# Two graph layers on one core: the second norm's output goes from the vector engine through SBUF and the DMA transpose, the second attention runs two graphs behind

## The chip, the cores and the metric

The kernel runs on one core of a Trainium2 chip, in one launch. The time is device time in microseconds (us), the median of several runs. The engines of the core work in parallel, each on its own queue in program order: TensorE (PE; its weight loads are listed as PEld), VectorE (DVE), ScalarE (ACT), GpSimd (POOL) and SyncE (SP), whose queue only issues DMAs here. They wait for each other on semaphores alone; nothing else orders them.

## What is computed

There are 32 graphs of 256 nodes with 512 features, float32. Each goes through a multi-head attention layer with an adjacency mask and then through a second, single-head graph attention, both behind a layer norm with relu and both added to their input:

```python
h = jnp.maximum(_layernorm(x), 0.0)
# L0: 16 heads of 32
q, k, v = heads(h @ Wq + bq), heads(h @ Wk + bk), heads(h @ Wv + bv)
scores = jnp.einsum('bhqd,bhkd->bhqk', q, k) * scale
scores = jnp.where(adj[:, None] == 0, -jnp.inf, scores)
x = x + (softmax(scores) @ v) @ Wo + bo
h = jnp.maximum(_layernorm(x), 0.0)
# L1: alpha from feature @ wq and feature @ wk
alpha = jnp.maximum((h @ wq) @ (h @ wk).T, 0.0) * (adj != 0)
x = x + softmax(alpha, axis=1) @ (h @ weight)
```

## The kernel before

**Tiles.** A graph is two row tiles of 128 nodes by 512. Every float32 factor is split into a high and a low float16 part, and a product is made of three matmuls (high by high, high by low, low by high). ACT writes the high part, DVE the low part (input minus high); for the attention weights POOL writes the low part (line 1115). `wm` is the product of the two second-layer attention matrices, made once at the start, so alpha is h2 wm h2^T: `g0`, `g1` make wm^T h2^T, `al` makes alpha, `hw0`, `hw1` make h2 times the weight, `av0`, `av1` the weighted sum.

**Stages.** The loop body (one for each graph t, all engines) has 16 steps, one for each head u. `weigh(u)` (PE lines 483 and 485, eight pairs of short products) stands at the start of step u+1; behind it a step holds the dense tiles that the table `DENSE` gives it, about as much PE work in each. `ROLE` says for which graph a tile is made in body t (0: t, 1: t+1, -1: t-1). `BANK` gives each tile one of three PSUM banks (`ring`); PE waits until DVE has finished the tile that had the bank before. `scores` of four heads stand at the ends of steps 11, 15, 3, 7. The first two bodies (t = -1 and 0) and the last ones are written out; 2 to 29 are a hardware loop. In body 0 the tiles of graph -1 are missing, and their places are used to make `wm` and the merged bias (`merge`, `merged_low`).

**A head.** DVE masks the scores (line 864, `mask`, four or five steps ahead), ACT takes the exponential (625) and the high part (638), POOL the low part (1115), and SP issues a DMA transpose of both parts (355, `turned`) at step u-1 of its own queue. PE's `weigh(u)` waits for its landing. DVE then sums high and low parts (877 and 879, `sum_parts`) for each pair of heads; `weigh` of the next even head waits for that, because it reuses the bank.

**The second norm.** In steps 2 and 3 DVE adds the products `wo0`, `wo1` to `x1` (963) and takes their statistics (883). In step 4 it makes mean and deviation (889, 907 to 911) and the normalised rows `work` (916, two passes). In step 5 PE turns them with eight float32 transposes through the identity (518, tiles `h2_0`, `h2_1`) between the halves of `v1`; ACT (649) and DVE (921) make relu's high and low part of them out of PSUM. `g0` follows in step 6.

**The first norm** goes another way: POOL normalises (1137), ACT and DVE split in SBUF (694, 921 `half`), and SP turns both parts with two DMA transposes (367, `transpose_h1`) in step 6, behind the `turned` of head 7. ACT issues the load of the next input `xa` (766) in step 5.

**The second softmax.** `al` ends in step 11. DVE masks alpha (981), takes the maximum (996), ACT the exponential (707), DVE the reciprocal (1004, 1007), ACT and DVE the parts `e` (718, 1012) in step 12; `av0`, `av1` stand in steps 14 and 15 of the same body, and DVE adds `x1` to them into `xo` (990), which SP stores in step 1 of the next body.

## Time and profile before

| what | value |
|---|---|
| median of 3 runs | 1568.2 us (1566.75 to 1570.06) |
| the profiled execution, as timed | 1570.8 us |
| its span in the profile | 1569.0 us |
| PE busy | 1504.6 us (96%) |
| DVE, ACT, POOL busy | 1247.9, 1128.3, 1064.8 us |
| DMA transposes | 512 of `turned`, 64 of `h`, all from SP |
| PE's granted clock, mean | 0.992 |

The rows further down are of four kinds. The page has one line for each engine with its busy time, share and number of instructions. A timeline row is: start in us, length in us, engine, line and operation, names written and read, shape, number of instructions merged, and in brackets the idle time of the engine before it and what ended it. A row of the windows view has a stretch, its length, each engine's busy time and number of instructions, the granted PE clock (1.00 is 2.4 GHz, 0.50 is 1.2 GHz), the busy share of the DMA engines and GB/s. A DMA issue row has what is moved, the issuing queue, the number, and the median us from issue to landing.

### The profile page before, as it was taken

The numbers are of one execution on the slowest core, as the hardware profiler recorded it, in microseconds if no ns is written. First come the engines' busy times: TensorE is split into PE (matmuls) and PEld (weight loads), VectorE is DVE, ScalarE is ACT, GpSimd is POOL, SyncE is SP. The second block draws the span as 40 slices with busy tenths as digits, with TensorE's granted clock in tenths as the row PEclk, the third lists the DMA queues.
The fourth block names the chain that finished last, engine by engine and source line by source line (L and its number), as shares of the span: only waits on it lengthen the run. The fifth ranks groups of instructions, "written<-read, shape, count | busy, mean of one in ns | idle before, by whom it ended". The sixth has DMA issues, their size and how long they took to land.

```text
span 1569.0 us, 50846 instructions
## 1 busy us (share of the span) xinstructions
PE 1504.6 (96%) x16561; PEld 1106.7 (71%) x16561; DVE 1247.9 (80%) x4042; ACT 1128.3 (72%) x2477; POOL 1064.8 (68%) x1478
## 2 busy tenths in 40 slices
PE   2889999999999999999999999999999999999996
PEld 1557777777777777777777777777777777777753
DVE  6778888887887878788888878888887888888763
ACT  2567777777777777777777777777777777777761
POOL 2466767777677777767677776777776777777650
PEclk9999999999999999999999999999999999999998
DMA  7647777667667766666776766777676677767760
GB/s 241 135 95 132 133 163 160 152 136 152 138 138 166 160 144 143 144 136 148 166 157 141 152 140 134 154 160 159 135 158 136 133 161 160 153 135 159 125 119 16
DMA packets 656198, 226.28 MB, mean 144 GB/s; under 512 B 611488, under 2 KB 627872, under 8 KB 656160
## 3 DMA queue, kind: packets, MB, share of 16 engines
q1 hardware_dynamic: 636848, 188.57, 59.1%
q10 hardware_dynamic: 19312, 37.23, 8.5%
q8 instruction: 21, 0.34, 0.1%
q14 instruction: 17, 0.14, 0.0%
HBM read 57.94 MB, written 16.78 MB: 48 GB/s over the span
## 4 chain that ended last, share of the span: by engine, by line
POOL 35%; issue 34%; PE 22%; DVE 4%; ACT 2%; DMA 1%; POOLq 1%; SPq 0%; ACTq 0%; DVEq 0%
PE ring L408 18%; POOL wv_raw L1115 16%; POOL heads_out L1149 6%; POOL x L1172 4%; POOL keep L1181 3%; POOL far L1190 3%; POOL xa L1137 1%; PE score L464 1%; PE pv L483 1%; DMA turned<-wv_raw 1%; POOL newton L1133 1%; PE ring L518 1%; PE pv L485 0%; DVE wk_raw L864 0%; DVE tops L785 0%
## 5 line engine op out<-in xcount | busy, mean ns | idle before, releaser
L1115 POOL TENSOR_TENSOR wv_raw<-wk_raw,wv_raw 128x512 f16<-128x512 f32 x512 | 608.0, 1190 | 362.8 <-ACT wv_raw L638 358.5
L625 ACT ACTIVATE wk_raw<-wk_raw,least 128x256 f32<-128x256 f32 x1024 | 459.0, 497 | 6.8 <-DVE least L864 6.8
L864 DVE CUSTOM_DVE_ANT_0 wk_raw<-score,far,undo_score 128x256 f32<-128x256 f32 x1024 | 444.0, 478 | 7.1 <-issue 5.1
L638 ACT ACTIVATE wv_raw<-wk_raw 128x512 f16<-128x512 f32 x512 | 320.5, 626 | 8.6 <-issue 4.5
L483 PEld LDWEIGHTS pv<-val,turned 128*128 128x128 f16 x2048 | 149.7, 97 | 67.4 <-issue 43.9
L483 PE MATMUL pv<-val,turned 128*128 128x65 f16 x2048 | 185.9, 192 | 10.8 <-DMA turned<-wv_raw 7.0
L408 PE MATMUL ring<-wv_hi,h 128*128 128x256 f16 x1024 | 189.3, 273 | 0.0
L408 PE MATMUL ring<-h,wq_hi 128*128 128x256 f16 x1024 | 176.3, 274 | 7.6 <-DVE wk_lo L827 7.6
L1149 POOL TENSOR_TENSOR heads_out<-o_sum,o_rcp 128x64 f32<-128x64 f32 x512 | 153.0, 320 | 42.6 <-DVE o_sum L879 42.6
L485 PE MATMUL pv<-val,turned 128*128 128x33 f16 x2048 | 178.1, 179 | 0.0
L408 PE MATMUL ring<-h,wk_hi 128*128 128x256 f16 x1024 | 176.6, 274 | 0.0
L485 PEld LDWEIGHTS pv<-val,turned 128*128 128x128 f16 x2048 | 136.1, 96 | 15.3 <-issue 1.3
L408 PE MATMUL ring<-h_hi,wm_hi 128*128 128x256 f16 x512 | 140.4, 274 | 2.0 <-DVE h_lo L921 1.6
L408 PE MATMUL ring<-h_hi,wm_lo 128*128 128x256 f16 x512 | 140.6, 275 | 0.0
L408 PE MATMUL ring<-h,wq_lo 128*128 128x256 f16 x512 | 140.5, 274 | 0.0
L408 PE MATMUL ring<-h_lo,wm_hi 128*128 128x256 f16 x512 | 140.5, 274 | 0.0
L408 PE MATMUL ring<-h,wk_lo 128*128 128x256 f16 x512 | 140.4, 274 | 0.0
L408 PE MATMUL ring<-wv_lo,h 128*128 128x256 f16 x512 | 140.0, 273 | 0.0
L408 PEld LDWEIGHTS ring<-h,wq_hi 128*128 128x128 f16 x1024 | 93.4, 98 | 24.5 <-DVE wk_lo L827 7.7
L408 PEld LDWEIGHTS ring<-wv_hi,h 128*128 128x128 f16 x1024 | 100.2, 98 | 14.2
L464 PE MATMUL score<-stage 32*128 32x256 f16 x3072 | 107.4, 270 | 1.7 <-DVE stage L942 1.2
L939 DVE SCALAR_TENSOR_TENSOR stage<-ring,bias_q,stage 128x256 f16<-128x256 f32 x128 | 61.6, 481 | 58.5 <-ACT stage L660 54.8
(151 smaller groups left out, 3570.6 us busy)
## 6 DMA issues: line engine op xcount, KB each, us to landing
xin<-x_dram ACTq DMA_DIRECT2D x32, 512.0 KB, 3.8
out_dram<-xo SPq DMA_DIRECT2D x32, 512.0 KB, 3.7
xa<-x_dram ACTq DMA_DIRECT2D x31, 512.0 KB, 4.2
adj_in<-adj_dram SPq DMA_DIRECT2D x32, 256.0 KB, 2.9
turned<-wv_raw SPq DMA_TRANSPOSE x512, 3.2
adjt_in<-adj_t_dram SPq DMA_DIRECT2D x32, 256.0 KB, 3.1
wq_raw<-wq_dram SPq DMA_DIRECT2D x2, 512.0 KB, 7.0
wk_raw<-wk_dram SPq DMA_DIRECT2D x2, 512.0 KB, 8.6
```

The costliest lines, as they stand in the source:

```text
L408: last = nc.tensor.matmul(dst, a, b, start=(k == 0 and s == 0), stop=(k == tiles - 1 and s == 2))
L464: last = nc.tensor.matmul(score[i][:, q * NODES:(q + 1) * NODES], stage[rows, g % 2, of_q, q * P:(q + 1) * P], stage[rows, g % 2, of_k, :] ...
L483: nc.tensor.matmul(pv4[:, slot, 0:VCOLS], turned[:, u % DEEP, q, 0, k, :], val[:, k, u, 0:VCOLS], start=(k == 0), stop=False)
L485: last = nc.tensor.matmul(pv4[:, slot, HEAD:VCOLS], turned[:, u % DEEP, q, 1, k, :], val[:, k, u, HEAD:VCOLS], start=False, stop=(k == QT ...
L625: last = nc.scalar.activation(probs[:, at, q, :], probs[:, at, q, :], ACT.Exp, bias=least[:, at, q:q + 1], scale=-1.0)
L638: nc.scalar.activation(halves[:, at, :, 0, :], probs[:, at, :, :], ACT.Copy).then_inc(hi["p"], 1)
L864: last = nc.vector.tensor_tensor_reduce(out=probs[:, at, q, :], in0=score[u % GROUP][:, q * NODES:(q + 1) * NODES], in1=far[:, q, :], scal ...
L939: nc.vector.scalar_tensor_tensor(out=stage[:, k % 2, 1, :], in0=src[:, 0:NODES], scalar=bias_q[:, k:k + 1], in1=stage[:, k % 2, 0, :], op0 ...
L1115: nc.gpsimd.tensor_tensor(halves[:, at, :, 1, :], probs[:, at, :, :], halves[:, at, :, 0, :], ALU.subtract).then_inc(lo["p"], 1)
L1149: last = nc.gpsimd.tensor_tensor(dst, o_sum[:, pair % 2, q:q + 3:2, :], o_rcp[:, pair % 2, q:q + 3:2].unsqueeze(2).broadcast_to([P, 2, HEAD]),
L1172: last = nc.gpsimd.tensor_tensor(x1[:, q, :], xin[:, q, :], out_bias[:], ALU.add)
L1181: last = nc.gpsimd.tensor_scalar(keep[:, q, :], adjt_in[:, q, :], 0, 0, ALU.is_equal, ALU.is_equal)
```

## The change

- **Second norm.** `work` is no longer turned by PE. ACT writes relu's high part of it (two instructions, step 4) and DVE its low part (two instructions, step 5) into `half2` in SBUF, and SP turns them with two DMA transposes (`transpose_h2`, step 5, between `turned` of head 6 and of head 7). `g` and `hw` wait for the landing of both (`h2_in`).
- **Table.** `v1` is whole in step 5; `av0`, `av1` stand in step 6 and belong to graph t-2; `g0` starts in step 7 as `g0a`; `g0b`, `g1a` in 8, `g1b`, `qk0a` in 9, `qk0b`, `hw0a` in 10, `hw0b`, `ot0` in 11, `al` whole in 12, `qk1` in 13, `v0a`, `hw1a` in 14, `hw1b`, `v0b` in 15. The softmax of alpha stands in step 13.
- **Residual.** SP copies `x1` to `xo` by DMA in step 12; DVE adds the attention's product to `xo` in place. The store moves from step 1 to step 8.
- **Buffers.** `g` and `hw` live in the space of the raw `wk1_t`.
- **Entry and end.** SP loads `wq` and `wv`, ACT loads `wk`; the first norm of graph 0 is made on DVE instead of POOL; eight small matmuls stand before the first product; the first product waits for the split of `wq` alone; the merges and scale searches of body 0 and the weight splits are dealt to other steps; the last two bodies have tables of their own (`DENSE_LAST`, `DENSE_END`).

```diff
-    ["v1a", "h2_0", "h2_1", "v1b"],
-    ["g0"],
-    ["g1a"],
-    ["g1b", "hw0a"],
-    ["hw0b", "qk0a"],
-    ["qk0b", "ala"],
-    ["alb", "ot0"],
-    ["hw1"],
+    ["v1"],
+    ["av0", "av1"],
+    ["g0a"],
+    ["g0b", "g1a"],
+    ["g1b", "qk0a"],
+    ["qk0b", "hw0a"],
+    ["hw0b", "ot0"],
+    ["al"],
     ["qk1"],
-    ["v0a", "av0"],
-    ["av1", "v0b"],
+    ["v0a", "hw1a"],
+    ["hw1b", "v0b"],
 ]
...
 AL_STEP = step_of("al")
+SOFTMAX_STEP = AL_STEP + 1
...
-VAR2 = 4
+VAR2, TURN2_STEP = 4, 5
...
-ADJ_STEP, STORE_STEP = 0, 1
+ADJ_STEP, STORE_STEP, KEEP_X_STEP = 0, 8, 12
...
             sp.dma_start(xa[:], x_v[0, :, :, :]).then_inc(xa_in, 16)
+            for half in range(2):
+                load_raw(sp, "wq", half)
...
+            def transpose_h2(b):
+                if started(b - 1):
+                    sp.wait_ge(mm["hw"], count(b - 1, 2, 1))
+                    sp.wait_ge(mm["al"], count(b - 1, 1, 0))
+                for q in range(QT):
+                    sp.wait_ge(lo["h2"], count(b, QT, q))
+                    settle(sp, sp_settled)
+                    sp.dma_start_transpose(
+                        h2[:, :, :, q * P:(q + 1) * P].rearrange("p h d n -> p (h d) n"),
+                        half2[:, q, :, :].rearrange("p h d -> p (h d)")).then_inc(h2_in, 16)
+
+            def keep_residual(b):
+                sp.wait_ge(added, count(b, 2, 1))
+                if started(b - 1):
+                    sp.wait_ge(stored, count(b - 1, 16, 15))
+                sp.dma_start(xo[:], x1[:]).then_inc(kept, 16)
...
                         transpose_probs(*head)
                     if s == TURN1_STEP and nxt:
                         transpose_h1(n)
+                    if s == TURN2_STEP and prev:
+                        transpose_h2(p)
+                    if s == KEEP_X_STEP and prev:
+                        keep_residual(p)
...
-                    pe.wait_ge(lo["h2"], count(b, 2, k))
+                    pe.wait_ge(h2_in, count(b, QT, QT - 1) * 16)
...
-                    for d in range(KT):
-                        last = nc.tensor.transpose(dst[:, d * P:(d + 1) * P],
-                                                   work[:, k, d * P:(d + 1) * P], ident[:])
-                    last.then_inc(mm["h2"], 1)
...
+            def second_half(q, b):
+                act.wait_ge(normed[1], count(b, QT, q))
+                if started(b - 1):
+                    act.wait_ge(h2_in, count(b - 1, QT, QT - 1) * 16)
+                nc.scalar.activation(half2[:, q, 0, :], work[:, q, :], ACT.Relu
+                                     ).then_inc(hi["h2"], 1)
...
+            def second_half(q, b):
+                dve.wait_ge(hi["h2"], count(b, QT, q))
+                relu_low(half2[:, q, 1, :], work[:, q, :], half2[:, q, 0, :], lo["h2"])
...
-                    if k == 0 and started(b - 1):
-                        dve.wait_ge(stored, count(b - 1, 16, 15))
+                    if k == 0:
+                        dve.wait_ge(kept, count(b, 16, 15))
                     nc.vector.scalar_tensor_tensor(out=xo[:, k, :], in0=src[:],
-                                                   scalar=undo_final[:, 0:1], in1=x1[:, k, :],
+                                                   scalar=undo_final[:, 0:1], in1=xo[:, k, :],
...
+                    if s == VAR2 + 1 and prev:
+                        for q in range(QT):
+                            second_half(q, p)
```

How the queues stand after it, at two places of the loop body. The first is SP's queue in steps 5 to 7; `turned` is a head's transpose, `h1` and `h2` the two norms'. The other instructions of the queue are the issuing engine's own waits and registers. Before, from head 7 on:

```order
L355 DMA_TRANSPOSE turned<-wv_raw 128x8x128 [waits lo_p,mm_pv]
L362 ISA
L363 ISA [waits mm_qk]
L365 ISA [waits mm_v]
L367 DMA_TRANSPOSE h1<-half1 128x8x128 [waits lo_h1]
L365 REGISTER_ALU
L367 DMA_TRANSPOSE h1<-half1 128x8x128 [waits lo_h1]
L348 REGISTER_ALU
L355 DMA_TRANSPOSE turned<-wv_raw 128x8x128 [waits lo_p,mm_pv]
```

The same place now:

```order
L412 ISA [waits mm_al,mm_hw]
L414 DMA_TRANSPOSE h2<-half2 128x8x128 [waits lo_h2]
L412 REGISTER_ALU
L414 DMA_TRANSPOSE h2<-half2 128x8x128 [waits lo_h2]
L384 REGISTER_ALU
L391 DMA_TRANSPOSE turned<-wv_raw 128x8x128 [waits lo_p,mm_pv]
L398 ISA
L399 ISA [waits mm_qk]
L401 ISA [waits mm_v]
L403 DMA_TRANSPOSE h1<-half1 128x8x128 [waits lo_h1]
L401 REGISTER_ALU
L403 DMA_TRANSPOSE h1<-half1 128x8x128 [waits lo_h1]
```

The two turns of `h2` stand ahead of head 7's, so four turns of norms instead of two lie between the low part of head 7 and the turn of head 8.

The second place is DVE's queue around the second softmax. `wk_raw,least<-score` is half a head's mask, `work<-ring,keep` the mask of alpha, `o_sum` a pair's sum. Before:

```order
L981 SCALAR_TENSOR_TENSOR work<-ring0,keep 128x512
L996 TENSOR_REDUCE l1_max<-work 128x2
L999 TENSOR_SCALAR l1_max<-l1_max,undo 128x2
L954 REGISTER_ALU
L955 TENSOR_TENSOR heads_t_lo<-ring1,heads_t_hi 128x512
L874 REGISTER_ALU
L877 RECIPROCAL o_rcp<-pv 128x4
L879 TENSOR_REDUCE o_sum<-pv 128x128
L1004 TENSOR_SCALAR l1_sum<-l1_sum 128x2
L1007 RECIPROCAL l1_rcp<-l1_sum 128x2
```

Now:

```order
L954 RECIPROCAL o_rcp<-pv 128x4
L956 TENSOR_REDUCE o_sum<-pv 128x128
L933 ISA
L937 REGISTER_ALU
L941 ISA wk_raw,least<-score0,far,undo_score 128x256
L941 ISA least 128x1
L941 ISA wk_raw,least<-score0,far,undo_score 128x256
L941 ISA least 128x1
L1058 SCALAR_TENSOR_TENSOR work<-ring2,keep 128x512
L1073 TENSOR_REDUCE l1_max<-work 128x2
L1076 TENSOR_SCALAR l1_max<-l1_max,undo 128x2
L1081 TENSOR_SCALAR l1_sum<-l1_sum 128x2
```

The pair's sum and head 0's mask now stand ahead of alpha's mask, and nothing stands between the maximum and the sum that waits for the exponential. Behind it come the masks of heads 1 and 2, `e_lo`, `qk1`'s low parts and the sum of the pair of heads 12 and 13.

## Rows read from the trace of the kernel before

**Rows 1.** The page: span, and PE with busy time, share and instructions.

```profile
span 1569.0 us, 50846 instructions
PE 1504.6 (96%) x16561; PEld 1106.7 (71%) x16561; DVE 1247.9 (80%) x4042; ACT 1128.3 (72%) x2477; POOL 1064.8 (68%) x1478
```

**Rows 2.** Windows view of one graph's period, and all transposes of line 518.

```profile
1131.86:1177.85 45.99, 45.97 (x519) 34.17 (x518) 37.70 (x125) 34.77 (x79) 33.28 (x47) 1.00 0.69 148
...
L518 PE MATMUL ring<-ident,work x256: 272/273/331, 117.8 to 1539.6; 128*128 128x128 f32 x128
```

**Rows 3.** PE's timeline: transposes, `v1b`, then the starts of steps 6, 9, 10.

```profile
1131.86 1.28 PE L518 MATMUL ring<-ident,work 128*128 128x128 f32 x8
...
1132.98 0.27 PE L408 MATMUL ring<-wv_hi,h 128*128 128x256 f16 x1
...
1134.29 0.19 PE L483 MATMUL pv<-val,turned 128*128 128x65 f16 x1
...
1142.62 0.20 PE L483 MATMUL pv<-val,turned 128*128 128x65 f16 x1
...
1145.46 0.19 PE L483 MATMUL pv<-val,turned 128*128 128x65 f16 x1
```

**Rows 4.** DVE's timeline, steps 1 to 5 of the same body.

```profile
1123.20 0.48 DVE L939 SCALAR_TENSOR_TENSOR stage<-ring,bias_q,stage 128x256 f16<-128x256 f32 x1 [0.77 <-ACT stage L660]
...
1133.22 1.29 DVE L921 SCALAR_TENSOR_TENSOR h_lo<-ring,h_hi 128x512 f16<-128x512 f32 x2
```

**Rows 5.** Timelines of SP and ACT, DMA issues with us to landing, h's minimum/median/maximum.

```profile
1134.95 1.23 SPq L367 DMA_TRANSPOSE h<-half  x1
...
1136.37 2.60 SPq L367 DMA_TRANSPOSE h<-half  x1
...
1139.22 5.93 SPq L355 DMA_TRANSPOSE turned<-wv_raw  x4
...
1134.81 0.39 ACTq L766 DMA_DIRECT2D xa<-x_dram  x1
...
h<-half SPq DMA_TRANSPOSE x1, 4.7
...
turned<-wv_raw SPq DMA_TRANSPOSE x4, 3.3
...
DMA to landing us min/median/max: 3.3/4.8/8.1
```

**Rows 6.** Timelines of PE and DVE, from alpha's end to step 15.

```profile
1149.83 0.27 PE L544 MATMUL ring<-ident,heads_out 128*128 128x128 f32 x1
...
1159.62 0.19 PE L483 MATMUL pv<-val,turned 128*128 128x65 f16 x1
...
1150.03 0.69 DVE L981 SCALAR_TENSOR_TENSOR work<-ring,keep 128x512 f32<-128x512 f32 x1 [1.01 <-PE ring L408]
...
1153.60 0.48 DVE L864 CUSTOM_DVE_ANT_0 wk_raw<-score,far,undo_score 128x256 f32<-128x256 f32 x1 [0.18 <-issue]
...
1154.65 0.88 DVE L1012 SCALAR_TENSOR_TENSOR e_lo<-work,l_rcp,e_hi 128x256 f16<-128x256 f32 x2 [0.15 <-ACT e_hi L718]
...
1156.05 0.47 DVE L864 CUSTOM_DVE_ANT_0 wk_raw<-score,far,undo_score 128x256 f32<-128x256 f32 x1
...
1158.66 0.17 DVE L877 RECIPROCAL o_rcp<-pv 128x4 f32<-128x4 f32 x1
...
1158.75 0.39 DVE L879 TENSOR_REDUCE o_sum<-pv 128x128 f32<-128x256 f32 x1
```

**Rows 7.** PE's timeline behind a wait near the end, and the windows view there.

```profile
1522.31 0.38 PE L408 MATMUL ring<-hw_hi,e_hi 128*128 128x512 f16 x1 [2.10 <-DVE hw_lo L970]
...
1522.91:1526.32 3.41, 3.41 (x17) 1.41 (x16) 0.75 (x1) 0.00 (x0) 0.47 (x2) 0.50 0.70 66
```

**Rows 8.** Timelines of ACT, DVE and PE at the entry.

```profile
10.57 1.06 ACT L694 ACTIVATE half<-xa 128x1024 f16<-128x1024 f32 x1 [3.95 <-POOL xa L1137]
...
24.50 2.48 DVE L827 SCALAR_TENSOR_TENSOR wq_lo<-wq_raw,scale,wq_hi 128x1024 f16<-128x1024 f32 x2 [1.12 <-ACT wq_hi L618]
...
29.43 0.61 PE L408 MATMUL ring<-h,wq_hi 128*128 128x256 f16 x2 [7.61 <-DVE wk_lo L827]
```

More of the change, by code:

```diff
@@ L84 @@
 HIGH1_STEP, LOW1_STEPS, TURN1_STEP = 14, (0, 2), 6
-VAR2 = 4
+VAR2, TURN2_STEP = 4, 5
 X1_STEP, XIN_STEP, KEEP_STEP, FAR_STEP = 1, 4, 4, 11
-ADJ_STEP, STORE_STEP = 0, 1
-SPARE = [tile(name) for name in ORDER if tile(name) in ("hw0", "hw1", "g0", "g1", "al", "av0")]
+ADJ_STEP, STORE_STEP, KEEP_X_STEP = 0, 8, 12
+JOBS = {"ot1": "bias", "wo1": 0, "av0": "turn", "av1": 1, "g0": "spread", "g1": 2, "hw0": 3,
+        "al": "turn", "hw1": "spread"}
+BATCH_OF = {"av0": 2, "g0": 2, "al": 3, "hw1": 3}
+SPARE = [tile(name) for name in ORDER if tile(name) in JOBS]
+MERGES = ["bias", 0, 1, 2, 3]
+WARM = 8
 LOADS = ("wq", "wk", "wv", "wk1_t", "wq1_t", "wo", "w1")
@@ L113, in started, with deal, bank_of, order @@
     return not (isinstance(graph, int) and graph < 0)
+def deal(t):
+    if isinstance(t, int) and t >= BATCH - 1:
+        return DENSE_LAST if t == BATCH - 1 else DENSE_END
+    return DENSE
+def bank_of(name, b):
+    if isinstance(b, int) and b == BATCH - 1 and ROLE[name] == -1:
+        return BANK_END[name]
+    return BANK[name]
 def bank_before(name, t):
-    at, shift = ORDER.index(name), 0
+    def order(body):
+        return [other for step in deal(body) for other in step if not other.endswith("b")]
+    body, at = t, order(t).index(name)
     while True:
@@ L121, in bank_before @@
         if at < 0:
-            at, shift = at + len(ORDER), shift - 1
-        other = ORDER[at]
-        if BANK[tile(other)] != BANK[tile(name)]:
+            body -= 1
+            at = len(order(body)) - 1
+        other = order(body)[at]
+        graph = body + ROLE[other]
+        if bank_of(tile(other), graph) != bank_of(tile(name), t + ROLE[name]):
             continue
-        graph = t + shift + ROLE[other]
-        if t + shift == 0 and tile(other) in SPARE:
+        if body == 0 and tile(other) in SPARE:
             return other, -1 - t
-        if t + shift < -1:
+        if body < -1:
             return None, 0
@@ L444, in merge @@
                                                 stop=(k == KT - 1))
-                else:
-                    for half in range(2):
-                        wait_raw(pe, "wo", half)
-                    for k in range(KT):
-                        last = nc.tensor.matmul(dst[:], bv_wide[:, k, :], raw["wo"][:, k, :],
-                                                start=(k == 0), stop=(k == KT - 1))
                 last.then_inc(merged, 1)
@@ L606, in body @@
                             scores(g, t)
+                    if nxt and not cur and s == SCORE_STEPS[0]:
+                        spread_scale(1, 1, pv)
             for name in ORDER:
-                assert len({bank_before(name, t) for t in range(2, BATCH - 2)}) == 1
+                assert len({bank_before(name, t) for t in range(2, BATCH - 1)}) == 1
             sweep(pe, body)
@@ L766, in body @@
                         act.dma_start(xa[:], x_v[n + 1, :, :, :]).then_inc(xa_in, 16)
+            for half in range(2):
+                load_raw(act, "wk", half)
             act.wait_ge(const_ok, 2)
@@ L1049, in body @@
                         first_low(1, n)
+                    if soften and not cur:
+                        second_low(p)
                     if s == LATE_MASK and cur:
```

233 lines of the change are left out of this document (134 added, 99 removed).

## The prediction

> **What bounds the kernel now.** The page comes first: PE is busy for 1504.6 of 1569.0 us, the next engine is at 80% [rows 1]. The windows view of one graph's period says how hard that bound is: in 45.99 us PE is busy for 45.97, at the full clock, while DVE has 37.70, ACT 34.77 and POOL 33.28 us of work [rows 2]. So a period is the sum of PE's issue times, and work taken off PE shortens it as long as nobody makes PE wait. The timelines say how close the others are behind. Head 8's turn is issued at 1139.22 and lands 3.3 us later, at 1142.5 [rows 5]; the products that wait for it start at 1142.62 [rows 3]. The sum of heads 12 and 13 ends at 1159.1 and PE wants it at 1159.62 [rows 6]. Both have slack of 0.1 and 0.5 us, so the order of the small queues matters as much as PE's work.
>
> **1. The eight transposes go.** They start at 1131.86, and `v1b` behind them at 1132.98 [rows 3]: 1.12 us of PE for each graph, 32 times (256 instructions, rows 2), 36 us in all if nothing else moves. ACT's and DVE's two instructions each stay about as long (DVE's two took 1.29 us out of PSUM [rows 4]) and stay at the same place of DVE's queue (ACT's come a step earlier). The rest of the dense work is only dealt anew.
>
> **2. A wait ahead of `g0a`.** When are the parts of h2 ready? DVE's last wait before them is in step 1, for `qk2` (1123.20); from there to the two passes at 1133.22 it works without a gap [rows 4]. The change alters nothing in between, and mask 9 still stands ahead, so the low parts end at about 1133.9 and 1134.5 as before. The first turn is issued at 1133.9. What two such turns take is seen at h1: the second is issued 1.42 us after the first, itself occupies the queue for 2.60 us and lands 4.7 us later [rows 5]. There ACT's 512 KB load of `xa` was issued at 1134.81, 0.14 us ahead of the first [rows 5]; in the new order it comes behind `v1`, which now ends 1.1 us earlier, and so falls on the first h2 turn again. Landing: 1133.9 + 1.4 + 4.7 = 1140.0; with the least that any turn of h took, 3.3 us, 1138.6 [rows 5]. PE gets there as follows: step 6 begins at 1134.29 - 1.12 = 1133.17; `av0`, `av1` fill a step (2.84 us, from 1142.62 to 1145.46 [rows 3]), and head 6's short products take some 0.25 us: 1136.3. So PE stands still for 2.3 to 3.7 us in every graph, more than the 1.12 us that it saved. Behind `g0a` come 5.2 us of work until head 8's products (1142.62 - 1.12 - 1136.3).
>
> **3. The turns of heads 7 and 8.** In SP's queue the two h2 turns stand ahead of head 7's, which was ready earlier, and h1's two stand behind that. Issue times: h2 at 1133.9 and 1135.3, head 7 at 1135.3 + 2.85 = 1138.2 (the step from 1136.37 to 1139.22 [rows 5]), then h1, h1 and head 8 at about 1.5 us each (four in 5.93 [rows 5]): 1142.7, landing at 1146.0. PE could be there at 1140.0 + 5.2 = 1145.2, so the turn decides: step 9 starts at 1146.0 instead of 1142.62, 3.4 us later, the saving included. Without the collision with `xa` all of it comes some 1.4 us earlier, 2.0 us later than before. The store that now stands behind head 8's turn can hold up head 9's by a few tenths more (512 KB, as long as xa's effect at most): upper end 4.1. I take 3.4, the collision being the row that is nearest.
>
> **4. A wait in step 15.** Before, `al` ended at 1149.83 and head 14's products stood at 1159.62 [rows 6], 9.8 us later. Now `al` ends with step 12, and head 14 stands two steps behind: 2 x 2.84 = 5.7 us. DVE's chain between them, counted from the end of `al`: alpha's mask starts 0.2 behind it (1150.03) and the first head mask 3.6 behind that (1153.60), since DVE waits for ACT's exponential meanwhile; then the masks of heads 1 and 2 and `qk1`'s parts, which took from 1156.05 to 1158.66, 2.6 with 0.2 of waiting in it; `e_lo`, 0.8; the pair's sum, 0.5 [rows 6]. That is 0.2 + 3.6 + 2.4 + 0.8 + 0.5 = 7.5 us against 5.7. The head mask and `hw_lo` that stood in the old chain are gone from it, and still it is too long. PE waits 1.8 us; with ACT a little quicker or slower 1.4 to 2.0; I take 1.7. DVE's idle time before it, while `al` was running, can't be used, since its queue is in order.
>
> **5. The moved residual, the store, the buffers.** `xo` needs the copy at step 6 of the next body, ten steps after its issue; two turns of heads behind it may be late by about a microsecond each, under step 15's wait. DVE's additions keep their length. I cost this at nothing; if that cover is gone, it is up to 0.7 us a graph.
>
> **6. Entry and end.** The first product started at 29.43, behind the low parts of `wk` [rows 8]. It now needs those of `wq` alone, one group of 2.48 us less, and the first norm no longer waits 3.95 us for POOL [rows 8] but for about 1.9 us of DVE (three small and two long instructions): together 4.5 us. Body 0's merges lie better spread, 1.5. At the end the first attention product fills gaps and `hw0`, `hw1` stand under the softmax, but the turn by DMA stands in the open: -2, give or take 3. Together -8, from -14 to -2.
>
> **7. The sum.** Steps 2 to 4 apply to bodies 1 to 30 or so, taken as 30: 30 x (3.4 + 1.7) = 153. Span 1569.0 + 153 - 8 = 1714. The profiled execution was timed 1.8 above its span and 2.6 above the median, so the median should be 0.8 below: 1713 us.
>
> **A rule that speaks against the change.** Rows 3 show eight transposes by PE in 1.12 us, rows 5 two DMA turns of as much data in 6.1 us from the first issue (1.4 and 4.7). The Trainium skill, page "VectorE: DVE Perf Modes", section "Rules for kernel authors", says to turn a 128x128 tile on TensorE if the target may be PSUM, and by the DMA crossbar otherwise. By that rule the change would lose wherever the landing isn't covered; the trace agrees on the order of the two.
>
> **The rivals.**
> - **The turns are covered and PE's saving stays** (faster). For it: `av0`, `av1` and head 6 stand between, 3.1 us. It decides at `g0a`: the second turn would have to land by 1136.3, and step 9 gains only while head 8's turn is there before 1142.6. For that DVE's passes would have to come over 2.3 us earlier, and SP's four extra microseconds of queue vanish. Against it: rows 4 and 5 throughout. Time: 1569.0 - 36 - 8 - 0.8 = 1524.
> - **Only the norm's wait is there**, step 15's isn't, because some link of DVE's chain overlaps that I counted one behind the other: 30 x 3.4 - 8: 1662; without the collision too (2.0), 1620.
> - **The clock falls in each graph.** Behind an idle time of 2.10 us PE ran 3.41 us at 0.50, that is 1.2 instead of 2.4 GHz [rows 7]; an idle time of 3.7 us in each graph would cost up to 1.7 us more each. Part of it hides under head 8's turn (0.8 us of room). With 1.7 in full and the upper ends of steps 3 and 4 (4.1 and 2.0): 30 x 7.8 - 8: 1794; more likely 30 x 6: 1740. The Trainium skill, page "TensorE: Matmul & The Clock Gate", Part 1, says that PE's clock is let through at half rate when PE has been idle and in full once it is busy; by that rule this rival holds in most graphs, and rows 7 agree for one place.
> - **The change doesn't do what it says**: not likely; the order of the queues shows the transposes gone and the DMAs there.
>
> **How the numbers follow.** Both waits, with or without some clock loss, 1680 to 1775: 0.65. Only the first wait, 1620 to 1680: 0.15. Above 1775: 0.08. Between 1570 and 1620 (both much smaller than reckoned): 0.03. Covered turns, about 1524: 0.08. No change: 0.01. The range leaves out the top and everything under 1620: 1620 to 1775. A measurement can tell about 0.2%, 3 us, from no change. Faster 0.08, same 0.01, slower 0.91.
>
> **What would show it.** Right: PE idle of 2.3 to 3.7 us ahead of `g0a`, released by the DMA of h2; head 8's products released by their turn; PE idle of about 1.7 us ahead of head 14's products, released by `o_sum`; a period near 51 us; PE's clock mean under 0.99. Wrong: a period of 45 us with PE busy throughout would mean that the low parts of h2 come earlier in DVE's queue than I think, or that the turns land faster; a period of 49 that only the first wait is real.

## The result, and the profile after

| what | before | after |
|---|---|---|
| median | 1567.5 us (1563.8 to 1570.1) | 1758.0 us (1756.8 to 1759.9) |
| span of the profiled execution | 1569.0 us | 1755.9 us |
| mean period of the loop, from weigh(0) to weigh(0) | 45.98 us | 52.07 us |
| PE's granted clock, mean | 0.992 | 0.957 |

The changed kernel takes 1.121 times as long (95% interval 1.119 to 1.123). The period was read over 29 graphs from the starts of `weigh(0)` in PE's timeline.

The page of after, its line on the engines, answers [rows 1]. PE has 237 instructions fewer, and yet it is busy for longer, since part of the time its clock is halved:

```profile
span 1755.9 us, 50712 instructions
PE 1529.4 (87%) x16324; PEld 1101.4 (63%) x16324; DVE 1272.8 (72%) x4054; ACT 1130.5 (64%) x2477; POOL 1066.7 (61%) x1470
```

PE's waits of after (engine and line, releaser: us in total, times, longest). The first row holds two waits of each graph, the second one:

```profile
PE pv L543 <- DVE o_sum L956: 91.9, 63, 4.9
PE ring L465 <- DMA h<-half: 79.8, 32, 7.2
```

The windows view of one period, against [rows 2]: 46.62 of 51.77 us are busy, where before it was 45.97 of 45.99.

```profile
1092.53:1144.30 51.77, 46.62 (x511) 33.86 (x509) 38.46 (x125) 34.88 (x78) 33.40 (x47) 0.97 0.68 152
```

PE's timeline of that body shows where it stands still. `weigh(5)` begins at 1106.84 (step 6), `weigh(6)` at 1110.86, `g0a` at 1113.62, `weigh(8)` at 1120.16 (step 9) and `weigh(14)` at 1139.06 (step 15). In brackets stands the idle time ahead of each and what ended it:

```profile
1110.86 0.20 PE L543 MATMUL pv<-val,turned 128*128 128x65 f16 x1 [1.05 <-DVE o_sum L956]
...
1113.62 0.39 PE L465 MATMUL ring<-h,wm_hi 128*128 128x256 f16 x2 [2.37 <-DMA h<-half]
...
1120.16 0.19 PE L543 MATMUL pv<-val,turned 128*128 128x65 f16 x1
...
1139.06 0.20 PE L543 MATMUL pv<-val,turned 128*128 128x65 f16 x1 [1.73 <-DVE o_sum L956]
```

The windows view behind the second wait: PE runs 3.41 us at 0.50, that is 1.2 instead of 2.4 GHz. Of graphs 1 to 30, 23 have one such stretch and 7 one of 6.83 us; before, none of them had any.

```profile
1114.28:1117.69 3.41, 3.41 (x42) 2.04 (x40) 0.00 (x0) 0.00 (x0) 0.00 (x0) 0.50 0.86 165
1117.70:1121.10 3.40, 3.40 (x39) 3.07 (x38) 3.32 (x13) 1.91 (x4) 1.40 (x3) 1.00 1.08 271
```

DVE's and POOL's timelines in steps 5 and 6, and the view of the tile `half` (ns minimum/median/maximum), answer [rows 4]. Of DVE's two low parts of h2 one takes 678 ns and the other 1574:

```profile
1106.82 2.17 DVE L998 SCALAR_TENSOR_TENSOR half<-work,half 128x512 f16<-128x512 f32 x2
...
L998 DVE SCALAR_TENSOR_TENSOR half<-work,half x2: 678/1126/1574, 1106.8 to 1108.3; 128x512 f16<-128x512 f32 x2
...
1106.69 1.16 POOL L1213 TENSOR_TENSOR wv_raw<-wk_raw,wv_raw 128x512 f16<-128x512 f32 x1 [0.99 <-ACT wv_raw L695]
```

SP's timeline, against [rows 5]: h2's turns, head 7's, h1's, head 8's. ACT's load of `xa` was issued at 1107.36; h2's two turns landed 3.9 and 3.7 us after their issue, head 8's 3.2, at 1119.45:

```profile
1108.49 2.69 SPq L414 DMA_TRANSPOSE h<-half  x2
1111.44 1.54 SPq L391 DMA_TRANSPOSE turned<-wv_raw  x1
1113.36 2.66 SPq L403 DMA_TRANSPOSE h<-half  x2
1116.28 1.24 SPq L391 DMA_TRANSPOSE turned<-wv_raw  x1
```

**Where the 6.09 us of a graph come from.** Means over the same 29 graphs: PE stands still for 5.2 us more, which are the three waits (1.05 ahead of `weigh(6)`, 2.40 ahead of `g0a`, 1.72 ahead of `weigh(14)`), and it is busy for 0.9 more (46.8 against 45.9). The transposes' 1.12 us (rows 3) are gone from the busy time, so something adds 2.0 to it. Most of that is the clock: from `g0a` to `weigh(8)` the same work takes 6.54 us in the rows above and 5.20 in x1 below, where the clock stays up; over all graphs the mean is 6.75, so the clock costs 1.5 us a graph. An estimate, half of the mean halved stretch ((23 x 3.41 + 7 x 6.83) / 30 = 4.21 us), would give 2.1 and is too high. Some 0.5 us of the busy time stay unattributed; part of it is `weigh`'s products, 4.25 us a graph against 3.92 before.

Over the whole span: up to `weigh(0)` of graph 1 it is 1.9 us less (102.4 before, 100.5 after), from there over 30 graphs to that of graph 31 180.3 more (1384.1 before, 1564.4 after), in graph 31 6.0 more, and 2.6 more behind its last head: 187.0, against 186.9 between the spans.

### The profile page after: what moved, and what is told of

Same layout as the page of the kernel before. It is cut to its first block, busy times and chain, and to the rows that moved or that the text cites. A ratio compares the mean times of both kernels' runs of the same rounds, so it can differ in the third digit from the quotient of the medians.

```text
span 1755.9 us, 50712 instructions
## 1 busy us (share of the span) xinstructions
PE 1529.4 (87%) x16324; PEld 1101.4 (63%) x16324; DVE 1272.8 (72%) x4054; ACT 1130.5 (64%) x2477; POOL 1066.7 (61%) x1470
## 4 chain that ended last, share of the span: by engine, by line
PE 49%; DVE 28%; DMA 8%; issue 8%; SPq 3%; ACT 3%; DVEq 1%; POOL 0%; ACTq 0%; POOLq 0%
PE ring L465 38%; DMA h<-half 6%; DVE wk_raw L941 6%; PE score L524 5%; DVE half L998 4%; PE pv L543 3%; DVE x L1040 2%; SPq L414 2%; DVE stage L1019 2%; DVE stage L1016 2%; PE ring L598 2%; ACT work L766 1%; DVE stats L960 1%; DVE work L1058 1%; DVE l_max L1073 1%
## 5 line engine op out<-in xcount | busy, mean ns | idle before, releaser
L1213 POOL TENSOR_TENSOR wv_raw<-wk_raw,wv_raw 128x512 f16<-128x512 f32 x512 | 617.7, 1209 | 356.6 <-ACT wv_raw L695 352.5
L465 PE MATMUL ring<-h,wm_hi 128*128 128x256 f16 x1024 | 210.0, 309 | 79.8 <-DMA h<-half 79.8
L738 ACT ACTIVATE wk_t_raw<-ring 128x512 f16<-128x512 f32 x64 | 38.2, 597 | 240.8 <-PE ring L465 240.8
L465 PE MATMUL ring<-wv_hi,h 128*128 128x256 f16 x1024 | 183.0, 272 | 0.9 <-DVE wv_lo L893 0.9
L465 PE MATMUL ring<-w_hi,h 128*128 128x512 f16 x512 | 174.4, 382 | 6.1 <-DVE heads_t_lo L1032 4.9
L465 PEld LDWEIGHTS ring<-h,wm_hi 128*128 128x128 f16 x1024 | 104.2, 109 | 103.4 <-DMA h<-half 70.4
L954 DVE RECIPROCAL o_rcp<-pv 128x4 f32<-128x4 f32 x256 | 44.8, 175 | 157.8 <-PE pv L545 157.1
L465 PE MATMUL ring<-h,wm_lo 128*128 128x256 f16 x512 | 158.7, 310 | 0.0
L524 PE MATMUL score<-stage 32*128 32x256 f16 x3072 | 120.6, 294 | 5.3 <-DVE stage L1019 4.1
```

What stands on the lines that cost most here:

```text
L465: last = nc.tensor.matmul(dst, a, b, start=(k == 0 and s == 0), stop=(k == tiles - 1 and s == 2))
L524: last = nc.tensor.matmul(score[i][:, q * NODES:(q + 1) * NODES], stage[rows, g % 2, of_q, q * P:(q + 1) * P], stage[rows, g % 2, of_k, :] ...
L738: nc.scalar.activation(gH[:, 2 * k:2 * k + 2, :], src[:].rearrange("p (c n) -> p c n", c=2), ACT.Copy).then_inc(hi["g"], 1)
L954: nc.vector.reciprocal(o_rcp[:, pair % 2, :], pv4[:, :, 2 * HEAD])
L1213: nc.gpsimd.tensor_tensor(halves[:, at, :, 1, :], probs[:, at, :, :], halves[:, at, :, 0, :], ALU.subtract).then_inc(lo["p"], 1)
```

## The experiments

All are variants of the changed kernel, and each time is a median of four to five runs, beside runs of the kernel before on the same chip (medians 1569 to 1572 us). "Period" is the mean from `weigh(0)` to `weigh(0)`.

### The clock: x1_fill

`FILL` is 8.

```diff
                 elif name.startswith("g"):
+                    if k == 0 and 0 in halves:
+                        for _ in range(FILL):
+                            nc.tensor.matmul(dst[:, 0:P], ident[:], ident[:], start=True,
+                                             stop=True)
                     pe.wait_ge(h2_in, count(b, QT, QT - 1) * 16)
```

> Changed kernel plus eight small products (128 columns through the identity, into the bank that g0a is about to fill anyway), issued ahead of g0a's wait for the turned h2; nothing else differs. They take about 1.7 us at the full clock and lie inside the 2.15 to 2.7 us for which PE stands still there. Theory (the clock falls behind the two waits of 1.05 and 2.4 us, and 3.4 to 6.8 us at half rate cost PE half of that): PE stays at 2.4 GHz behind g0a, and weigh(8) would come 1.7 us earlier; head 8's turn lands 0.7 us before weigh(8) starts in the changed kernel, so it takes 1.0 of it back unless it moves too. Period 0.7 to 1.7 us shorter, 1706 to 1737 us in all. Rival 1 (the waits alone make the time, the clock's loss is hidden under other waits): 1755 to 1760. Rival 2 (the eight products themselves delay g0a): slower, up to 1770.

Measured: 1735.0 us (1732.9 to 1737.6), clock 0.992, period 51.31. The waits of its PE:

```profile
PE pv L544 <- DMA turned<-wv_raw: 31.2, 36, 1.9
PE ring L466 <- DMA h<-half: 20.3, 30, 5.4
```

The windows view from `g0a` to `weigh(8)`, where PE is busy for 5.20 us, at the full clock, and waits for the rest:

```profile
1100.33:1106.34 6.01, 5.20 (x68) 4.11 (x69) 3.31 (x13) 1.91 (x4) 1.46 (x4) 1.00 0.96 205
```

With PE kept busy no graph from 2 to 30 has a halved stretch, and the kernel gains 23 us, 0.76 a graph. That is the lower end of what was expected: a new wait of 0.8 us on head 8's turn stands at `weigh(8)`. In the changed kernel that turn was 0.7 us early only because the slow clock had kept PE away. So the clock's fall is real, and of its 1.5 us the queue of turns masks about half.

### The wait in step 15: x2_e_late

```diff
-                    if soften and cur:
+                    if s == SOFTMAX_STEP + 1 and prev and cur:
                         second_low(p)
```

> Changed kernel with DVE's low part of the second softmax (e_lo, 0.8 us) taken out of the chain ahead of the sum of heads 12 and 13 and put behind it. Theory (step 15's wait of 1.72 us is the length of DVE's chain, link by link): the wait falls to about 0.9 us and the period by 0.8, 1734 us. Rival (head 14's own turn or mask stands close behind the sum, so that the wait only changes its name): 1750 to 1760.

Measured: 1732.5 us (1730.2 to 1736.1), period 51.25, and the wait, in PE's timeline, 1.04 instead of 1.72:

```profile
1126.95 0.20 PE L543 MATMUL pv<-val,turned 128*128 128x65 f16 x1 [1.04 <-DVE o_sum L956]
```

The time is what was expected, but not all of it comes from the wait: this shrank by 0.68, not by the 0.8 that `e_lo` takes, and the rest of the 0.82 us a graph goes with the clock, which here has no stretch of 6.83 us in graphs 2 to 30. The wait does hang on DVE's chain.

### The wait ahead of `g0a`: x3_half_first, x4_mask_late

```diff
+                    if s == VAR2 + 1 and prev:
+                        for q in range(QT):
+                            second_half(q, p)
                     for by in MASKS_AHEAD[s % GROUP][:1 if s == LATE_MASK else 2]:
...
-                    if s == VAR2 + 1 and prev:
-                        for q in range(QT):
-                            second_half(q, p)
```

> Changed kernel with DVE's two low parts of h2 put ahead of the mask of head 9 in step 5. The turns of h2 can be issued some 0.8 us earlier. Theory (g0a waits for DVE's passes and two turns one behind the other): g0a's wait shrinks by the same 0.7 to 0.9, the wait of 1.05 us in step 7 stays, period 0.8 shorter if head 8's turn moves along, 1733 us. Rival (ACT's high parts or SP's queue hold the turns, not DVE): no change, 1755 to 1760.

Measured: 1717.1 us (1716.5 to 1717.6), period 50.79, which neither the theory (1733) nor the rival (1755 to 1760) had. It gained 1.28 a graph, not 0.8, and the wait that vanished was the other one, that of 1.05 ahead of `weigh(6)`. The tile view and PE's timeline:

```profile
L998 DVE SCALAR_TENSOR_TENSOR half<-work,half x2: 677/678/679, 1133.2 to 1133.8; 128x512 f16<-128x512 f32 x2
...
1139.98 0.39 PE L465 MATMUL ring<-h,wm_hi 128*128 128x256 f16 x2 [2.40 <-DMA h<-half]
```

Both passes now take 0.67 to 0.69 us, in all 32 graphs; in the changed kernel one of them took 1.57 to 1.64 us in 31. The held pass is the one that begins while POOL's low part of a head is already running (1106.82 against 1106.69, rows above): in the changed kernel all 31 that began so were held, and none of the other 33. Here both begin before POOL does. The 0.9 us that come back are what DVE's sum of heads 4 and 5 had been late by; the rest of the gain goes with the clock, which falls in 25 of graphs 2 to 30 and in none of them for 6.83 us. The turns could be issued 1.7 us earlier, but now `xa`'s load fell on them (issued 0.57 us behind the first), and they landed after 5.3 and 4.5 us instead of 3.9 and 3.7; so the wait ahead of `g0a` stayed at 2.40 with PE itself 0.9 earlier there.

The second test leaves everything and changes only which of two instructions of DVE is first in step 6:

```diff
-                    if s == LATE_MASK and cur:
-                        mask(s + 5, t)
...
                         sum_parts(s // 2 - 1, t)
+                    if s == LATE_MASK + 1 and cur:
+                        mask(s + 4, t)
```

> Changed kernel with the mask of head 10 put behind the sum of heads 4 and 5 on DVE, so that weigh(6), which now waits 1.05 us for that sum, gets it some 0.8 us earlier. Theory (what ends last is the landing of h2, and the wait of 1.05 us only stands in front of the same landing): the 1.05 goes to about 0.2 and g0a's wait grows by as much, 1755 to 1760 us, no change. Rival (the two waits add up): 1733 us. A clock that falls once more or once less behind a single wait of 3.4 us would show as up to 50 us either way.

Measured: 1761.0 us (1758.2 to 1761.8), period 52.11. The waits:

```profile
PE ring L465 <- DMA h<-half: 105.0, 32, 7.3
PE pv L543 <- DVE o_sum L956: 65.8, 63, 3.9
```

26 us went from the one row to the other, and the time stayed. The wait of 1.05 alone cost nothing; it stood in front of the same landing.

### The new table without the new route: x5_pe_turn

```diff
-    ["v1"],
+    ["v1a", "h2_0", "h2_1", "v1b"],
     ["av0", "av1"],
...
-                        transpose_h2(p)
...
-                    pe.wait_ge(h2_in, count(b, QT, QT - 1) * 16)
+                    pe.wait_ge(lo["h2"], count(b, 2, 1))
```

> Changed kernel with only the second norm's route undone: h2 is turned by PE again (eight transposes between the halves of v1 in step 5), ACT and DVE split it out of PSUM, and no DMA turns h2; av0 and av1 swap banks. Table, residual, entry and end stay as changed. Theory (the DMA route makes the two waits of steps 7, the clock's fall and nothing else; the new table makes step 15's wait): no PE idle ahead of g0a, none ahead of weigh(6), since a pass out of PSUM is not held up by POOL; clock mean 0.99; step 15's wait stays at 1.7. Period 45.85 + 1.72 = 47.6, in all 1616 to 1622 us. Rival (the new table alone makes the waits): period 50 or more, above 1690.

Measured: 1623.6 us (1621.4 to 1626.8), clock 0.991, period 47.89. No wait ahead of `g0a` or `weigh(6)`, 1.73 in step 15:

```profile
PE pv L542 <- DVE o_sum L966: 57.4, 34, 2.5
...
L1008 DVE SCALAR_TENSOR_TENSOR h<-ring,h x64: 678/690/692, 117.4 to 1598.6; 128x512 f16<-128x512 f32 x64
```

This splits the loss: the route by DMA costs 134 us of the 190, the table with its step 15 most of the rest. The low part read out of PSUM never took more than 692 ns, in 64 passes, but that doesn't test what held the pass, since POOL has no pass at the same time as any of them. The changed kernel itself has the test, in the additions to `xo`: 128x512 as well, one input in PSUM and one in SBUF. 60 of the 64 begin while POOL is in a low part, some as close behind its start as the held pass. None took more than 751 ns, and POOL's passes there keep their 1.16 us each. The tile view, and DVE's and POOL's timelines:

```profile
L1067 DVE SCALAR_TENSOR_TENSOR xo<-ring,undo_final,xo x64: 730/737/751, 173.9 to 1752.0; 128x512 f32<-128x512 f32 x64
...
1111.53 1.40 DVE L1067 SCALAR_TENSOR_TENSOR xo<-ring,undo_final,xo 128x512 f32<-128x512 f32 x2
...
1111.39 2.27 POOL L1213 TENSOR_TENSOR wv_raw<-wk_raw,wv_raw 128x512 f16<-128x512 f32 x2
```

### The load of `xa` and the turns: x7_xa_late, x8_xa_early

```diff
-XA_STEP, SCALE_STEP = 5, 6
+XA_STEP, SCALE_STEP = 6, 6
```

> As x3_half_first (DVE's low parts of h2 ahead of head 9's mask), and ACT's 512 KB load of xa one step later, so that it no longer falls on the turns of h2 (in x3 they landed after 5.31 and 4.52 us, in the changed kernel after 3.94 and 3.66). Theory (the load and the turns share the DMA engines): the second turn lands 0.8 us earlier, g0a's wait falls from 2.40 to about 1.6, period about 50.0 and, if the clock no longer falls behind the shorter wait, 48.3; in all 1693 us, or 1640. Rival (xa doesn't matter): 1717 us as x3.

Measured: 1770.1 us (1767.2 to 1774.3), period 52.47, slower than the changed kernel and outside everything that was expected. About 7 us of it are at the entry, where the scores of graph 0 now wait; the rest is in each graph. ACT's order moved the load by only 1.0 us, onto the second turn, which landed after 5.9 us; DMA issues in that stretch (median us to landing) and PE:

```profile
xa<-x_dram ACTq DMA_DIRECT2D x1, 512.0 KB, 5.3
h<-half SPq DMA_TRANSPOSE x2, 5.3
...
1131.33 0.61 PE L465 MATMUL ring<-h,wm_hi 128*128 128x256 f16 x2 [3.83 <-DMA h<-half]
```

My expectation had the place of the load wrong. That the load and the turns get in each other's way it had right, and the run shows it more strongly than x3. x8 issues the load ahead of the second norm's root in step 4 instead:

```diff
+                    if s == VAR2 and later:
+                        act.wait_ge(lo["h1"], count(n, QT, QT - 1))
+                        act.dma_start(xa[:], x_v[n + 1, :, :, :]).then_inc(xa_in, 16)
                     if s == VAR2 and prev:
                         root(1, p)
```

> As x3_half_first, with ACT's load of xa issued in step 4 ahead of the root of the second norm, some 3 us before the first turn of h2, instead of 0.57 us behind it (x3: landings 5.31 and 4.52, g0a's wait 2.40 us) or 0.17 us behind the second (x7: 4.60 and 5.93, wait 3.83). Theory (a turn that shares its flight with the load lands 1.2 to 2.6 us later; every turn costs about 3.2 without it): landings 3.3 to 3.5, g0a's wait 1.2 to 1.6, period shorter than x3's by 0.8 to 1.2, 1680 to 1693 us; if the clock no longer falls behind a wait that short, down to 1635. Rival (the landings in x3 and x7 are set by something else, such as the turns one behind the other): 1717 us.

Measured: 1683.2 us (1680.5 to 1688.3), clock 0.986, period 49.57. The total is in the range and the reason isn't. The load now follows that of `xin` by 2.7 us, and both met the turns of heads 4 to 6. SP's timeline, the landing of head 5's turn, and PE:

```profile
1107.07 5.10 SPq L391 DMA_TRANSPOSE turned<-wv_raw  x3
...
turned<-wv_raw SPq DMA_TRANSPOSE x1, 9.3
...
1117.93 0.20 PE L543 MATMUL pv<-val,turned 128*128 128x65 f16 x1 [2.68 <-DMA turned<-wv_raw]
```

PE waits 2.68 us at `weigh(5)` here, and `g0a` doesn't wait, because PE comes late. From graph to graph it differs: `weigh(5)` waits for nothing up to 3.0 us, 1.3 on the mean, and where it waits little, `g0a` waits up to 1.5. So the loads cost whichever turn they meet: 3.1 us to landing alone, up to 5.9 with one load beside it (x7), 9.3 with two.

### Do the mends add up? x6_all, x9_all_early

x6 takes x1, x3 and x7 together, x2 with the mask of head 2 behind the sum as well, and h1's turns behind head 8's:

```diff
-HIGH1_STEP, LOW1_STEPS, TURN1_STEP = 14, (0, 2), 6
+HIGH1_STEP, LOW1_STEPS, TURN1_STEP = 14, (0, 2), 7
...
+                    if s == SOFTMAX_STEP + 1:
+                        head = ahead(s - 1, 5, t, cur, nxt)
+                        if head:
+                            mask(*head)
```

> Changed kernel with every small mend at once: low parts of h2 ahead of head 9's mask, xa's load one step later, h1's turns behind head 8's turn, eight filling products ahead of g0a's wait, DVE's e_lo and the mask of head 2 behind the sum of heads 12 and 13. Theory (the parts add up): PE work 44.9, g0a's wait 1.6, step 15's wait about 0.2, no clock loss: period 46.7, in all 1568 + 30 x 0.7 + 3 = 1592 us. Rival (h2's landing by DMA can be hidden by such small moves after all): below 1570. Rival (a new wait for head 8 or 9): 1610 or more.

Measured: 1703.9 us (1700.7 to 1705.8), period 50.00, over 100 us above the theory. They did not add up: the load met the turns (wait ahead of `g0a` 1.74 behind 1.7 us of filling), the entry lost 7 us, and step 15's wait stayed at 1.04, although a mask was taken out of its chain. DVE's timeline says why: another link moved up, ACT's part of `qk1`.

```profile
1132.67 0.39 PE L466 MATMUL ring<-h,wm_hi 128*128 128x256 f16 x2 [1.74 <-DMA h<-half]
...
1104.66 0.48 DVE L1021 SCALAR_TENSOR_TENSOR stage<-ring,bias_q,stage 128x256 f16<-128x256 f32 x1 [0.80 <-ACT stage L717]
```

x9 is x8 with x1, x2 and that `TURN1_STEP`.

> x8_xa_early, and with it e_lo behind the sum of heads 12 and 13 (x2), the eight filling products (x1), and h1's turns behind head 8's. Theory (the parts add up once no load meets a turn): PE work 44.9, g0a's wait 1.2 to 1.6 filled and at full clock, step 15's wait 1.04: period 47.2 to 47.6, in all 1605 to 1620 us; still slower than before, since the first turn can't be issued before DVE's passes are through. Rival (another turn is met by a load or queues behind h2's): 1650 or more, as x6.

Measured: 1677.4 us (1674.1 to 1680.6), period 49.59: the rival. In a graph PE is busy for 47.1 us, some 1.8 of it filling that is of no use any more, and stands still for 2.5, of which 1.3 ahead of `weigh(5)` on the mean and 1.0 in step 15.

### More work between the low parts and `g0a`: r1, r2, r3

```diff
-    ["v1"],
-    ["av0", "av1"],
-    ["g0a"],
-    ["g0b", "g1a"],
-    ["g1b", "qk0a"],
-    ["qk0b", "hw0a"],
-    ["hw0b", "ot0"],
-    ["al"],
-    ["qk1"],
-    ["v0a", "hw1a"],
-    ["hw1b", "v0b"],
+    ["hw1"],
+    ["v1"],
+    ["av0"],
+    ["av1", "g0a"],
+    ["g0b", "qk0a"],
+    ["qk0b", "g1a"],
+    ["g1b", "ot0"],
+    ["qk1"],
+    ["al"],
+    ["v0a", "hw0a"],
+    ["hw0b", "v0b"],
```

> The DMA route with a table that puts enough PE work between DVE's low parts and g0a: hw1 of graph t-2 in step 5, v1 in 6, av0 in 7, av1 and g0a in 8, al in 13, softmax in 14, hw0 in 14 and 15. Low parts of h2 ahead of the mask of head 9, xa's load and h1's turns one step later. Theory (PE's 1.12 us is saved once h2's landing is covered and the sum of heads 12 and 13 stands ahead of the softmax on DVE): period 44.9 to 45.3, in all 1535 to 1550 us, below the kernel before. Rival (head 7's or 8's turn or the DVE chain of steps 0 to 6 is as late as before and now binds, since PE comes there 1.12 us earlier): period 46 to 47, 1568 to 1600.

Measured: 1779.2 us (1773.8 to 1786.0), period 52.92, the slowest of all and outside both ranges. `g0a` didn't wait, but `weigh(7)` did, 3.6 us on the mean, behind a turn that `xa`'s load had met (5.2 us to landing), and the softmax, one step later in the table, now held up the sum ahead of `weigh(0)`, 1.57 us. The clock fell in all of graphs 1 to 30, in more than half of them for 6.83 us or longer. PE's timeline:

```profile
1145.91 0.20 PE L545 MATMUL pv<-val,turned 128*128 128x65 f16 x1 [2.99 <-DMA turned<-wv_raw]
```

r2 deals that anew. Its main lines:

```diff
-    ["g0b", "qk0a"],
-    ["qk0b", "g1a"],
+    ["g0b", "g1a"],
+    ["qk0"],
     ["g1b", "ot0"],
-    ["qk1"],
-    ["al"],
+    ["qk1a", "ala"],
+    ["alb", "qk1b"],
...
+                    if s in (TURN2_STEP, TURN2_STEP + 1) and prev:
+                        transpose_h2(p, s - TURN2_STEP)
...
+                    if s == VAR2 and later:
+                        act.wait_ge(lo["h1"], count(n, QT, QT - 1))
+                        act.dma_start(xa[:], x_v[n + 1, :, :, :]).then_inc(xa_in, 16)
```

> r1_redeal mended where its trace showed waits (weigh(7) 3.0 us behind a turn that xa's load had met; weigh(0) 1.6 us behind DVE's sum, which stood behind ACT's late parts of hw0 and the softmax): xa's load in step 4, head 7's turn between the two of h2, head 8's ahead of h1's; g0b and g1a in step 9, qk0 in 10; al in the middle of steps 12 and 13, exponentials of alpha in step 14, its reciprocal and parts in 15. Theory (each wait was one of order, and PE's work without the eight transposes is 44.9 us): period 44.9 to 45.6, in all 1535 to 1560 us. Rival (DVE's chain of steps 0 to 6 holds masks and turns as late as before, so that the 1.12 us can't be had): period 46.0 or more, 1568 to 1620.

Measured: 1724.3 us (1722.1 to 1734.2), period 51.17, again outside both ranges: `weigh(5)` waits some 1.5 for a turn that both loads met, `weigh(0)` 2.21 for DVE's sum behind `e_lo`, with the clock down in 24 of graphs 1 to 30. r3 goes on from there. It also gives `g1` and `qk0` their banks of r1 back and puts ACT's `e_hi` behind the high parts of the dense tiles:

```diff
-X1_STEP, XIN_STEP, KEEP_STEP, FAR_STEP = 1, 4, 4, 11
+X1_STEP, XIN_STEP, KEEP_STEP, FAR_STEP = 1, 12, 4, 11
...
-                    if soften and not cur or s == SOFTMAX_STEP + 1 and prev and cur:
+                    if soften and not cur:
                         second_low(p)
+                    if s == 1 and present[-2]:
+                        second_low(t - 2)
```

> r2_redeal mended at the four waits of its trace, 4.9 us a graph: the load of xin goes from step 4 to step 12, so that xa's load has the DMA engines to itself beside the turns of heads 5 and 6 (these landed after 6.6 to 7.9 us, weigh(5) waited 1.51 and weigh(8) 0.81); e_hi on ACT goes behind the high parts of hw0 and v0, e_lo on DVE to step 1, behind the sum of heads 14 and 15 (weigh(0) waited 2.21 for it); g1, qk0 and qk1 take the banks of r1 (0.39). Theory (the DMA engines and the order of DVE's queue made every wait; with PE's work at 44.9 us the eight transposes' 1.12 us is then really saved): period 44.9 to 45.5, in all 1532 to 1555 us. Rival (a chain of another engine is as long as the old period and binds): 45.9 or more, 1565 to 1600.

Measured: 1669.1 us (1667.8 to 1670.8), clock 0.994, period 49.52; 1.062 of before (1.060 to 1.064). Its page and waits:

```profile
PE 1487.1 (89%) x16324; PEld 1067.5 (64%) x16324; DVE 1295.4 (78%) x4054; ACT 1115.3 (67%) x2477; POOL 1054.0 (63%) x1470
issue 34%; POOL 26%; SPq 12%; PE 9%; DVE 9%; DMA 7%; ACT 2%; POOLq 1%; DVEq 0%; ACTq 0%
...
PE pv L545 <- DVE o_sum L958: 69.7, 64, 2.5
PE pv L545 <- DMA turned<-wv_raw: 44.4, 40, 2.3
PE ring L600 <- POOL heads_out L1249: 18.8, 29, 0.7
```

It is the fastest variant with the new route, 89 us below the changed kernel. h2's landing is hidden and the clock stays up; PE's busy time, 1487.1, is below that of before (1504.6), by 17.5 us; the other half of the 36 us that the transposes took doesn't show in it, since `weigh`'s products, with waits ahead of them, read 4.4 us a graph instead of 3.9. What is left is 4 waits of 0.7 to 1.4 us in each graph, on DVE's sums, on a turn and on POOL. (The shares of the chain that ended last say little here: PE has 9%, but only 22% in the kernel before, where it is busy throughout.) My expectation had taken each wait as one of order alone, and even its rival, up to 1600, was too low. It fell: a table in which no other queue comes late wasn't found, and whether there is one is open.

## Why the prediction came out as it did

The direction and the range (1620 to 1775) held; the time was 1713 forecast and 1758 measured, 45 us too low. By its steps:

- **Step 1, the transposes: right, as far as PE's work goes.** They are gone (rows 2, page of after), 1.12 us of PE a graph, and where the clock stays up about half of it shows as less busy time (r3). That DVE's passes stay about as long was wrong for one of the two, 1.57 us instead of 0.68.
- **Step 2, the wait ahead of `g0a`: right in size and place, with two errors that cancelled.** Forecast 2.3 to 3.7 from a landing 6.8 us behind the start of step 6; measured 6.7 (1106.84 to 1113.57), and 1.05 + 2.40 = 3.5 of waiting. But the turns were issued 0.9 later than forecast, since a low part was held up beside POOL, and landed 1.0 us sooner, since `xa`'s load came 1.1 us ahead of them and not upon them. That the wait still came out at the upper end of the forecast is luck. The part at `weigh(6)` wasn't foreseen. x4 shows that it makes no difference which of the two it is.
- **Step 3, the turn of head 8: the size right, the reason wrong.** Forecast: landing 12.8 behind the start of step 6, and this decides. Measured: 12.6 (1119.45), but `weigh(8)` came at 13.3, later than its turn, since PE was at half its clock behind `g0a`. Step 9 starts 3.9 us later than before against a forecast of 3.4. x1 takes the clock's loss away, and then the turn decides, as forecast.
- **Step 4, step 15: right.** 1.72 against 1.7, released by `o_sum`. From the end of `al` (1131.50) to the end of the sum (1139.00) it is 7.5 us, as forecast, and the wait is there in x5 too, where nothing of the new route is left. DVE's timeline has the links:

```profile
1131.70 0.69 DVE L1058 SCALAR_TENSOR_TENSOR work<-ring,keep 128x512 f32<-128x512 f32 x1 [0.83 <-PE ring L465]
...
1138.60 0.40 DVE L956 TENSOR_REDUCE o_sum<-pv 128x128 f32<-128x256 f32 x1
```

  What the sum of lengths doesn't tell is what a shorter chain would give: `e_lo`'s 0.8 taken out gave 0.68 (x2), the mask's taken out as well gave nothing more (x6), since ACT's part of `qk1` came next.
- **Step 5: right.** No wait of PE or DVE on the copied residual or the store, and one of SP on the store, 2.5 us at the very end.
- **Step 6: wrong, by 15 us with the last graph (forecast -8, measured 0.4 - 2.4 + 6.0 + 2.6 = 6.6).** The first product started at 26.36 instead of 29.43 (rows 8), 3.1 of the 4.5 forecast, but PE then stood still for 4.10 us ahead of the scores, and `weigh(0)` of graph 0 was no earlier than before (48.4 against 48.0):

```profile
26.36 0.39 PE L465 MATMUL ring<-h,wq_hi 128*128 128x256 f16 x2 [0.87 <-DVE wq_lo L893]
...
35.82 1.47 PE L524 MATMUL score<-stage 32*128 32x256 f16 x24 [4.10 <-DVE stage L1019]
...
33.50 0.29 ACT L757 ACTIVATE newton<-meanvar,eps 128x2 f32<-128x2 f32 x1 [6.69 <-DVE meanvar L966]
```

  ACT stood behind DVE's statistics for 6.69 us. Body 0 gave 2.4. The end took 8.6 instead of giving 2. In the last bodies PE stands still for 4.85 us for DVE's low part of `heads_t`, which the prediction hadn't at all, and for 7.22 us for the turn by DMA, where before it stood for 3.82 and 1.65 around the transposes:

```profile
1706.04 0.61 PE L465 MATMUL ring<-w_hi,h 128*128 128x512 f16 x1 [4.85 <-DVE heads_t_lo L1032]
...
1730.28 0.58 PE L465 MATMUL ring<-h,wm_hi 128*128 128x256 f16 x2 [7.22 <-DMA h<-half]
```

  I had not looked for who comes next behind the first product.
- **Step 7, the sum: the missing term is the clock.** 30 x 5.1 became 30 x 6.01. The prediction had the fall of the clock as a rival (1740 for it), from one wait of 2.10 us in rows 7, and gave it up to 1.7 us a graph. It came in every graph, and 0.76 of its 1.5 us are left once the turns have masked their share (x1). A wait of that size had been shown to do it; it should have stood in the sum. These 23 us and the 15 of step 6 make most of the 45 us that were missing. The rule of the Trainium skill that was cited for this rival (page "TensorE: Matmul & The Clock Gate", Part 1) is borne out by this trace, where the clock was halved behind the waits in each graph.
- **The other rivals.** "Covered" fails on the landing, as rows 4 and 5 said: even r3 had to deal the whole table anew and move two loads for it. "Only the norm's wait" fails on step 15.

The held pass is the one mechanism that neither the prediction nor its rivals had, and it goes against the sentence at the start of this document that nothing but semaphores orders the engines. The Trainium skill, page "SBUF — State Buffer", section "Who interferes with whom", says that a DVE instruction with two SBUF inputs contends with a GpSimd instruction that reads SBUF, and that the one issued second is blocked until the first is through. The traces agree: 1574 ns against 678 where POOL had started first (0.90 us more, of 1.03 that POOL's pass still had to run), POOL's own pass up from 1.16 to 1.43 us or 1.62 (x3) where DVE had, and no effect with one of the inputs in PSUM (the additions to `xo`). That the two hold each other up is measured here; by what means no run shows. The move of `work` from PSUM to SBUF as DVE's input was in the diff, and the prediction took the pass as "about as long". The kernel before had a sign of it: its first norm has both inputs in SBUF, and of its 64 low parts the longest, at 52.81 behind the start of a POOL pass at 52.76, took 1658 ns. Its tile view:

```profile
L921 DVE SCALAR_TENSOR_TENSOR half<-xa,half x64: 673/698/1658, 11.7 to 1448.4; 128x512 f16<-128x512 f32 x64
```

## What to carry to other kernels

Where one engine is busy all the time, work that leaves it must come back as a wait on something that is later than that work took: here 1.12 us of PE against 5 us from DVE's last pass to the landing. Count the transfers that share the stretch before adding one, loads on other queues too, and in which order they queue; single mends here moved the wait to the next turn, and five of them together (x9) gave 81 us of 190 back. r3, with the table dealt anew as well, gave 89. When an operand moves from PSUM to SBUF, look whether the instruction now has two inputs there and what POOL does at that time.
